# AdaLN block on one core: attention probabilities kept unsplit in fp32, context and row sums on column tiles of 32

## Chip, core and metric

The kernel runs on one core of a Trainium2 chip. The metric is the time of one execution on the device in microseconds (us). The measured times are the median of three runs, 688.05 us, with 682.75 and 689.03 us as the lowest and highest.

## What is computed

The reference is one transformer block with adaptive layer norm on x of shape (8, 512, 256). Cut to what matters:

```python
mod = (silu(c) @ wmod).reshape(8, 6, 1, 256)      # shift, scale and gate, twice
h = layernorm(x) * (1 + ca) + sa
# inner block, 16 heads of 16 columns, window of 128 keys
g = layer_norm(h, ln1)
q, k, v = g @ Wq + bq, g @ Wk + bk, g @ Wv + bv
scores = einsum('blhd,bmhd->bhlm', q, k) * 0.25 + bias   # key j allowed where i-128 <= j <= i
attn = softmax(scores)
ctx = einsum('bhlm,bmhd->blhd', attn, v)
h = h + ctx @ Wo + bo
h = h + gelu(layer_norm(h, ln2) @ W1 + b1) @ W2 + b2     # 256 -> 1024 -> 256
x = x + ga * h
# second half: layer norm, shift and scale, mix with the previous token, then
out = sigmoid(xr @ Wr.T) * (square(relu(xk @ Wk.T)) @ Wv.T)
x = x + gb * out
```

## The kernel before

The five engines each run an instruction list written out by hand; semaphores tie them together. TensorE is called PE below, VectorE DVE, ScalarE ACT, GpSimd POOL, and SP is the queue that issues most transfers.

**Units.** The work is cut into 16 units `u` (8 batches times 2 halves of the heads) and, for the later layers, 16 half batches `i`. One unit of attention has four calls `gp = 4u + j`. Each call holds two heads: the key axis of a stationary tile interleaves the two heads (even partitions for one, odd for the other), so 64 keys of two heads fill 128 partitions. A call's scores fill eight key tiles `s`, each seen by a window of up to 192 queries, 1344 query columns in all. They lie with keys on partitions and queries along the row, unnormalised.

**One call before.** `scores(gp)` on PE (split fp16 operands stacked along the contraction, L325) writes PSUM; `exps` on ACT (L874, L879) writes `p32[gp % 2]` in fp32; `select` on POOL (L1927 to L1932) zeroes what is outside the window; `high_p` on ACT (L889) rounds it to fp16 as `p_hi`; `low_p` (DVE L1373 for j = 0 and 3, POOL L1940 for j = 1 and 2) writes the rest `p_lo`. `context(gp)` on PE (L350) multiplies 28 blocks of 128 x 128 probabilities, as the stationary operand, with 66 or 34 columns of `v_blk`, which holds the fp16 halves of v and a column of ones for the row sums. The output has queries on partitions. `normalise(gp)` on DVE (L1384, L1385, L1390) inverts the row sums, adds the two halves and writes `cx`. After four calls `transposes_c(u)` on PE (L361, four fp32 transposes of 128 columns) and `context_t(u)` on ACT (L914) turn `cx` into `ct` with channels on partitions, which `out_project` (L377) reads. v itself is split by `split_v` (ACT L859) and `rest_v` (DVE L1346).

**Maxima.** `maxima(u, qt)` finds a bound for the exponent. It issues fp16 products on 32 x 32 tiles: row tile j, column tile qb. For qt = 0 the first loop (L289) gives 256, 192, 128 and 64 columns for qb = 0 to 3 (four products each, one per j), the second loop (L293) 64, 128, 192 and 256, in this order:

```python
tiles = [(qt * P + qb * QB, quad[qb * QB:(qb + 1) * QB, j, :], slice(2 * HD * j, 2 * HD * (j + 1)))
         for qb in range(4) for j in range(HQ)]
```

**Buffers that couple the engines.** There are two slots of `p32`, `p_hi` and `p_lo`. Four PSUM banks (`quad`, the ring `ring_s`) are shared by projections, values, scores, maxima (which take all four), and transposes. The ring `ring_c` is one bank, for the context. `ring_b` and `ring_f` serve the later layers.

**Order.** Between the start-up (about the first 200 us) and the drain, a loop over batches interleaves scores, maxima and contexts of one unit with `up`, `down`, `receptance`, `keys` and `values_b` of earlier half batches. `warm` issues matmuls on an identity (L230) that fill waits in the start-up. On SP, `stacks(u)` issues 24 transfers of q and k per unit (L2163, L2165), `load_v` four per half (L2174).

## Time and profile before

| | |
|---|---|
| median of 3 runs | 688.05 us |
| profiled execution | 686.02 us, span 684.3 us |
| PE busy | 589.2 us (86%) |
| DVE busy | 509.6 us (74%) |
| ACT busy | 508.7 us (74%) |
| POOL busy | 366.8 us (54%) |
| granted TensorE clock, mean | 0.974 of 2.4 GHz |

PE's busy time counts the modelled end of every matmul, which reaches past the start of the next, so the pace of a stream of matmuls is read from start to start, not from the mean duration. The clock was at half speed only in stretches of the first 200 us and at the very end (0.88 on average in the first 100 us, 1.00 from 200 us to 600 us). Waits are named by the instruction that waited and the one that released it. Two times are used for a transfer: the time its issue takes on the queue, and the time from issue to landing.

### The profile page before, as it was taken

To read this page: it belongs to the slowest core of one execution; us is meant where nothing else is said; L and a number is where in the kernel's file an instruction comes from. 1 tells how busy PE (TensorE), PEld (TensorE's weight loads), DVE (VectorE), ACT (ScalarE), POOL (GpSimd) and SP (SyncE) were. 2 spreads that over 40 slices of the span, in tenths; PEclk is the share of its full clock that TensorE was granted. 3 is DMA by queue.
4 is the path that set the end of the run, shared out by engine and by line. 5 is a ranking of instruction groups with operands and counts; after the bars stand their busy time and mean duration, and the time that the engine had idled before them with its cause. 6 is when DMAs were issued, how large, how long until landed. Compare 5 with 4: busy or idle time off the path is not lost.

```text
span 684.3 us, 18053 instructions
## 1 busy us (share of the span) xinstructions
PE 589.2 (86%) x6814; PEld 470.4 (69%) x6814; DVE 509.6 (74%) x1058; ACT 508.7 (74%) x780; POOL 366.8 (54%) x514
## 2 busy tenths in 40 slices
PE   5686697998789898899889898989898988899986
PEld 2555586877577676767676767677777766777775
DVE  5576577777788788788888888888987687564563
ACT  2623755579698979897989888998898886894642
POOL 5202444481639554865677475937593657564231
PEclk9878999999999999999999999999999999999999
DMA  3734212232023032403232223222311332101010
GB/s 129 276 72 102 64 43 48 62 100 67 19 67 98 18 89 55 117 24 86 65 79 72 73 66 82 80 60 64 76 57 46 73 72 64 32 2 48 31 39 32
DMA packets 56867, 47.05 MB, mean 69 GB/s; under 512 B 26235, under 2 KB 48061, under 8 KB 56782
## 3 DMA queue, kind: packets, MB, share of 16 engines
q1 hardware_dynamic: 53798, 43.85, 23.9%
q10 hardware_dynamic: 2984, 2.05, 1.2%
q8 instruction: 55, 0.90, 0.6%
q14 instruction: 30, 0.25, 0.1%
HBM read 18.11 MB, written 4.23 MB: 33 GB/s over the span
## 4 chain that ended last, share of the span: by engine, by line
PE 39%; ACT 29%; issue 10%; DVE 9%; SPq 7%; DMA 3%; POOL 2%; ACTq 0%; DVEq 0%; POOLq 0%
ACT bank L942 6%; ACT p L874 5%; SPq L2163 4%; PE bank L230 4%; SPq L2165 4%; ACT hid_hi L952 3%; PE bank L425 3%; PE bank L463 3%; PE bank L451 3%; PE bank L426 3%; PE bank L427 3%; ACT L942 3%; PE quad L325 3%; ACT kt_hi L846 2%; DVE nmax L1359 2%
## 5 line engine op out<-in xcount | busy, mean ns | idle before, releaser
L1927 POOL TENSOR_SCALAR_AFFINE_SELECT p<-p 128x448 f32<-128x448 f32 x64 | 40.4, 632 | 218.7 <-ACT p L874 179.1
L874 ACT ACTIVATE p<-quad,scale_s 128x768 f32<-128x768 f32 (+1 forms) x102 | 81.9, 821 | 39.6 <-PE quad L325 28.5
L889 ACT ACTIVATE p_hi<-p 128x1344 f16<-128x1344 f32 x64 | 83.9, 1322 | 14.3 <-POOL p L1932 7.1
L1940 POOL TENSOR_TENSOR p_lo<-p,p_hi 128x1344 f16<-128x1344 f32 x32 | 87.6, 2736 | 5.0 <-ACT p_hi L889 5.0
L325 PE MATMUL quad<-q_st,k_st 100*128 100x192 f16 (+3 forms) x576 | 61.4, 229 | 22.4 <-ACT p L874 7.6
L1359 DVE TENSOR_REDUCE nmax<-quad 128x8 f32<-128x1032 f32 x64 | 78.9, 1234 | 2.2
L408 PE MATMUL bank<-bt_hi,w_hi 128*128 128x256 f16 x256 | 70.5, 275 | 9.5 <-DVE hid_lo L1432 8.3
L1432 DVE SCALAR_TENSOR_TENSOR hid_lo<-bank,inv_f,hid_hi 128x512 f16<-128x512 f32 x64 | 48.0, 749 | 37.8 <-ACT hid_hi L952 37.6
L425 PE MATMUL bank<-w_hi,hid_hi 128*128 128x256 f16 x256 | 70.0, 274 | 0.9 <-DVE hid_lo L1432 0.8
L409 PE MATMUL bank<-bt_lo,w_hi 128*128 128x256 f16 x256 | 70.2, 274 | 0.0
L410 PE MATMUL bank<-bt_hi,w_lo 128*128 128x256 f16 x256 | 70.2, 274 | 0.0
L942 ACT ACTIVATE bank<-bank,bias,scale_g 128x256 f32<-128x256 f32 x128 | 63.5, 537 | 8.6 <-PE bank L410 8.4
L426 PE MATMUL bank<-w_lo,hid_hi 128*128 128x256 f16 x256 | 69.8, 273 | 0.0
L427 PE MATMUL bank<-w_hi,hid_lo 128*128 128x256 f16 x256 | 69.8, 273 | 0.0
L325 PEld LDWEIGHTS quad<-q_st,k_st 100*128 100x128 f16 x576 | 42.7, 97 | 37.9 <-issue 11.1
L350 PE MATMUL bank<-v_blk,p_hi 128*128 128x66 f16 x896 | 55.2, 195 | 2.3 <-DVE cx L1390 1.4
L350 PE MATMUL bank<-v_blk,p_lo 128*128 128x34 f16 x896 | 57.0, 181 | 0.0
L1356 DVE COPY_PREDICATED quad<-later,quad 128x248 f32<-128x248 int16 x64 | 26.7, 417 | 37.9 <-PE quad L293 37.6
L350 PEld LDWEIGHTS bank<-v_blk,p_hi 128*128 128x128 f16 x896 | 45.2, 97 | 8.2 <-issue 4.3
L1373 DVE TENSOR_TENSOR p_lo<-p,p_hi 128x1344 f16<-128x1344 f32 x32 | 49.6, 1549 | 1.2 <-ACT p_hi L889 1.2
L230 PE MATMUL bank<-ident 128*128 128x128 f32 x322 | 50.5, 313 | 0.0
L230 PEld LDWEIGHTS bank<-ident 128*128 128x128 f32 x322 | 45.7, 222 | 3.0 <-issue 1.9
(226 smaller groups left out, 1636.7 us busy)
## 6 DMA issues: line engine op xcount, KB each, us to landing
k_st<-kt_hi SPq DMA_DIRECT2D x120, 64.0 KB, 2.0
v_blk<-vn SPq DMA_DIRECT2D x64, 66.0 KB, 2.2
x<-x SPq DMA_DIRECT2D x16, 256.0 KB, 2.8
out<-x SPq DMA_DIRECT2D x16, 256.0 KB, 2.1
q_st<-qt_hi SPq DMA_DIRECT2D x120, 32.0 KB, 1.9
k_st<-kt_lo SPq DMA_DIRECT2D x60, 64.0 KB, 2.0
xa<-x SPq DMA_DIRECT2D x7, 512.0 KB, 4.5
stage<-w_ff SPq DMA_DIRECT2D x2, 1024.0 KB, 8.0
```

The source lines that it names most:

```text
L230: e.matmul(psum[5][:, 0:P], ident[:, :], ident[:, :], start=True, stop=True)
L325: last = e.matmul(bank[:, c0:c0 + w], k_st[0:MR, half, j, s * P:(s + 1) * P], q_st[0:MR, half, j, s * KW + q0:s * KW + q0 + w], start=True ...
L350: last = e.matmul(dst[:, :, v0:VW], p[:, c:c + P], v_blk[:, half, s, :, j * VW + v0:(j + 1) * VW], start=(i == 0), stop=(i == len(pieces) ...
L408: e.matmul(dst, w1_hi[:, k, ms], bt_hi[:, k, :], start=(k == 0), stop=False)
L425: e.matmul(dst, hid_hi[:, m, ts], w2_hi[:, m, :], start=(m == 0), stop=False)
L426: e.matmul(dst, hid_hi[:, m, ts], w2_lo[:, m, :], start=False, stop=False)
L427: last = e.matmul(dst, hid_lo[:, m, ts], w2_hi[:, m, :], start=False, stop=(m == MF - 1))
L874: e.activation(p32[gp % 2][:, c0:c0 + 2 * w].rearrange("p (n c) -> p n c", n=2), quad[:, b0:b0 + 2, 0:w], ACT.Exp, scale=scale_s[:, 1:2]). ...
L889: e.activation(p_hi[gp % 2][:, :].rearrange("p (n c) -> p n c", c=GW)[:, :, 0:QW], p32[gp % 2][:, :].rearrange("p (n c) -> p n c", c=QW), ...
L942: e.activation(dst, dst, ACT.Gelu_apprx_tanh, bias=bias_1[:, m:m + 1], scale=scale_g[:, 0:1]).then_inc(s_gl, 1)
L1359: e.tensor_reduce(nmax[:, :, :, qt].rearrange("p a j -> p j a"), quad[:, :, 2 * QB - 2:2 * WIN].rearrange("p j (c a) -> p j a c", a=2), AX ...
L1940: e.tensor_tensor(cut(p_lo), p32[gp % 2][:, :].rearrange("p (n c) -> p n c", c=QW), cut(p_hi), ALU.subtract).then_inc(s_plp, 1)
```

## The change

Probabilities are no longer split. `high_p`, both `low_p`, `split_v`, `rest_v`, `normalise`, `transposes_c` and `context_t` are gone, and so are `p_hi`, `p_lo` and `cx`; `p32` has six slots. The roles of the operands in `context` are exchanged: v is the stationary operand (128 x 32, fp32), the probabilities are streamed (fp32, up to 192 columns at a time), and the output has channels on partitions already. `context(q)` handles a pair of calls. Its two value products write partitions 32j to 32j+31 of one bank, that is column tile j of the array, for two of the four j; the two products with `sel` (ones, for the row sums of each head, repeated over 16 rows) write the other two column tiles in a bank of `ring_s`.

The row sums then go a long way: `copy_den` (ACT) to SBUF, `fold_den` (SP, a transfer that lays one row of every 16 out as 128 x 32), `divide` (DVE, reciprocal), `save_den` (SP, to DRAM), `spread_den` (SP, back to 128 x 512, each row repeated 16 times), and `scale_c` (DVE) multiplies the context bank by it into `ct`. `scale_c` frees the one context bank. `copy_v` (ACT, two instructions per two token tiles) replaces the split of v. All five engines' lists are written in a new order, and the weights' columns for v and Wo's rows are reordered on the host.

```diff
-    VW = 2 * HD + 1
+    VW = 4 * HD
+    SLOTS = 6
...
+        den_rows = nc.dram_tensor("den_rows", (NU, 8, L), F32, kind="Internal").ap()
...
-        vn = sb("vn", [P, NT, 4, HQ * VW], F16)
-        v_blk = sb("v_blk", [P, 2, 8, 2, HQ * VW], F16)
+        vn = sb("vn", [P, NT, 2, 2, 2 * VW])
+        v_blk = sb("v_blk", [P, 2, 8, 2 * VW])
...
-        p32 = [sb(f"p32_{i}", [P, PW]) for i in range(2)]
-        p_hi = [sb(f"p_hi{i}", [P, 7 * GW], F16) for i in range(2)]
-        p_lo = [sb(f"p_lo{i}", [P, 7 * GW], F16) for i in range(2)]
-        rsum = sb("rsum", [P, NT, 2])
+        p32 = [sb(f"p32_{i}", [P, PW]) for i in range(SLOTS)]
...
-            def context(gp):
...
-                for t in range(NT):
-                    dst = bank[:, t * 2 * VW:(t + 1) * 2 * VW].rearrange("p (a w) -> p a w", a=2)
...
-                        last = e.matmul(dst[:, :, v0:VW], p[:, c:c + P], v_blk[:, half, s, :, j * VW + v0:(j + 1) * VW],
-                                        start=(i == 0), stop=(i == len(pieces) - 1))
...
+            def context(q):
...
+                if pair == 0:
+                    bank, free = ring_c.take(("av", u), s_ct, u + 1)
+                    e.wait_ge(s_vin[half], 4 * DMA * (u // 2 + 1))
+                    hold(e, *free)
+                den, free = ring_s.take(("den", q), s_dc, q + 1)
...
+                e.wait_ge(s_sel, 2 * q + 2)
                 hold(e, *free)
...
+                for s in (0, 3, 6, 1, 2, 4, 5, 7):
+                    c, w = {6: (6 * QW + KW, 2 * KW), 7: (6 * QW, KW)}.get(s, (s * QW, QW))
+                    for i in range(2):
+                        j = 2 * pair + i
+                        e.matmul(bank[32 * j:32 * j + 32, s * KW:s * KW + w], v_blk[:, half, s, 2 * j * HD:2 * (j + 1) * HD],
+                                 p32[(2 * q + i) % SLOTS][:, c:c + w], start=(s == 0), stop=(s == 7))
+                    for i in range(2):
+                        j = (2 * pair + i + 2) % HQ
+                        last = e.matmul(den[32 * j:32 * j + 32, s * KW:s * KW + w], sel[:, :],
+                                        p32[(2 * q + i) % SLOTS][:, c:c + w], start=(s == 0), stop=(s == 7))
                 last.then_inc(s_av, 1)
-
-            def transposes_c(u):
...
+            def copy_den(q):
...
+                rows = slice(0, 64) if q % 2 else slice(64, 128)
+                e.wait_ge(s_av, q + 1)
+                hold(e, s_rc, DMA * (q - 1))
+                e.activation(dn[rows, :], ring_s.at["den", q][rows, :], ACT.Copy).then_inc(s_dc, 1)
...
-                if first == 0 and gp >= 2:
-                    e.wait_ge(*low_of(gp - 2))
+                if first == 0:
+                    hold(e, s_av, (gp - SLOTS) // 2 + 1)
...
-            def high_p(gp):
...
-            def context_t(u):
...
-            def normalise(gp):
...
+            def divide(u):
...
+                e.wait_ge(s_rc, 2 * DMA * (u + 1))
+                e.reciprocal(rc[:, :], rc[:, :]).then_inc(s_rr, 1)
+
+            def scale_c(u):
...
+                e.wait_ge(s_rb, DMA * (u + 1))
+                hold(e, s_wo, 2 * (u // 2))
+                e.tensor_tensor(ct[:, u % 2, :], ring_c.at["av", u][:, :], rb[:, :], ALU.mult).then_inc(s_ct, 1)
...
+            def fold_den(q):
...
+                e.wait_ge(s_dc, q + 1)
+                hold(e, s_rs, DMA * u)
+                e.dma_start(rc[64 * pair:64 * pair + 64, :], dn[r0:r0 + 64:HD, :]).then_inc(s_rc, DMA)
+
+            def save_den(u):
...
+                e.wait_ge(s_rr, u + 1)
+                e.dma_start(den_rows[u], rc[:, :]).then_inc(s_rs, DMA)
+
+            def spread_den(u):
...
+                e.wait_ge(s_rs, DMA * (u + 1))
+                hold(e, s_ct, u)
+                e.dma_start(rb[:, :], den_rows[u].rearrange("r (o c) -> r o c", o=1).broadcast_to([8, HD, L])).then_inc(s_rb, DMA)
```

**Where instructions stand.** PE before, in the loop over batches: one context call with what stands around it (up to 66 and 34 columns of v, 28 products).

```order
L377 MATMUL quad<-wo,ct 128x256 x4
L350 MATMUL bank<-v_blk,p_hi 128x66 x2
L350 MATMUL bank<-v_blk,p_lo 128x2x17 x2
L350 MATMUL bank<-v_blk,p_hi 128x66 x4
L350 MATMUL bank<-v_blk,p_lo 128x2x17 x4
L350 MATMUL bank<-v_blk,p_hi 128x66 x4
L350 MATMUL bank<-v_blk,p_lo 128x2x17 x4
L350 MATMUL bank<-v_blk,p_hi 128x66 x4
L350 MATMUL bank<-v_blk,p_lo 128x2x17 x4
L325 MATMUL quad<-q_st,k_st 128x192
L325 MATMUL quad<-q_st,k_st 128x96 x2
```

PE after, in the loop over batches: the end of the projection of one unit, `receptance`, and the first of the two context calls of a unit; `p_2` and `p_3` are two of the six probability slots.

```order
L252 MATMUL quad<-at_hi,wa_lo 128x512
L439 MATMUL bank<-wb,mixed 128x256 x4
L318 MATMUL quad<-q_st,k_st 128x192 x4
L344 MATMUL bank<-p_2,v_blk 32x192
L344 MATMUL bank<-p_3,v_blk 32x192
L348 MATMUL quad<-p_2,sel 32x192
L348 MATMUL quad<-p_3,sel 32x192
...
L344 MATMUL bank<-p_2,v_blk 32x64
L344 MATMUL bank<-p_3,v_blk 32x64
L348 MATMUL quad<-p_2,sel 32x64
L348 MATMUL quad<-p_3,sel 32x64
L318 MATMUL quad<-q_st,k_st 128x192
```

Four products on four column tiles now stand behind each other, eight times per call; there are two such calls per unit where there were four calls and a group of transposes.

DVE before, in the loop: the three instructions of `normalise` stand behind each maximum or so; they wait for PE's context call (`av`).

```order
L1359 TENSOR_REDUCE nmax<-quad 128x4x2 [waits mov]
L1384 RECIPROCAL rsum<-bank 128x8 [waits cx_s,av]
L1385 TENSOR_REDUCE bank<-bank 128x128
L1390 TENSOR_TENSOR cx<-bank,rsum 128x8x16 [waits ctr,cs]
L1444 SCALAR_TENSOR_TENSOR x<-bank,scale_y,x 128x512 [waits b2_s,f2]
```

DVE after: the reciprocal waits for two folding transfers (`rc_in`), the product for the spreading transfer (`rb_in`); three other instructions stand between, and the next maximum stands behind.

```order
L1536 RECIPROCAL rc<-rc 128x32 [waits rc_in]
L1568 TENSOR_TENSOR bt_lo<-bank,bt_hi 128x512 [waits bth]
L1595 SCALAR_TENSOR_TENSOR x<-bank,scale_y,x 128x512 [waits b2_s,f2]
L1649 SCALAR_TENSOR_TENSOR tr<-tr,bank 128x512 [waits r,vb]
L1543 TENSOR_TENSOR ct<-bank,rb 128x512 [waits wo_s,rb_in]
L1520 COPY_PREDICATED quad<-later,quad 128x4x62 [waits mxm,mtt]
L1523 TENSOR_REDUCE nmax<-quad 128x4x2 [waits mov]
```

SP after, in the loop: the two folds of a unit, the save and the spread, with the loads of v and of the gates between; the stacks of the next unit stand behind all of them.

```order
L2461 DMA rc<-dn 64x1x32 [waits rs,dc]
L2452 DMA v_blk<-vn 64x4x128 [waits av,v3]
L2452 DMA v_blk<-vn 64x4x128 x3
L2461 DMA rc<-dn 64x1x32 [waits rs,dc]
L2467 DMA den_rows<-rc 128x32 [waits rr]
L2491 DMA mod_g<-mod_rows 128x256 [waits yg,gates_out]
L2474 DMA rb<-den_rows 128x1x512 [waits ct_s,rs]
```

Four transfers per unit (two folds, save, spread) are new on this queue.

## Rows read from the trace of the kernel before

**Rows 1.** The page, part 1: busy time, share and instructions of each engine.

```profile
PE 589.2 (86%) x6814; PEld 470.4 (69%) x6814; DVE 509.6 (74%) x1058; ACT 508.7 (74%) x780; POOL 366.8 (54%) x514
```

**Rows 2.** The page, part 4: the chain that ended last, shares by engine.

```profile
PE 39%; ACT 29%; issue 10%; DVE 9%; SPq 7%; DMA 3%; POOL 2%; ACTq 0%; DVEq 0%; POOLq 0%
```

**Rows 3.** Windows, one batch of the loop: busy us and counts, clock, DMA.

```profile
283.00:353.70 70.70, 64.26 (x810) 50.90 (x794) 60.36 (x124) 61.75 (x96) 45.33 (x63) 1.00 0.27 70
```

**Rows 4.** Waits of PE: instruction, releaser, total us, times, longest.

```profile
PE quad L293 <- ACT p L874: 12.7, 19, 1.1
PE bank L408 <- DVE hid_lo L1432: 8.3, 16, 1.4
PE quad L325 <- ACT p L874: 7.6, 13, 0.9
...
PE quad L361 <- DVE cx L1390: 6.5, 9, 1.2
```

**Rows 5.** Timeline of PE: start, us; a context call and what follows.

```profile
297.21 0.23 PE L350 MATMUL bank<-v_blk,p_hi 128*128 128x66 f16 x2
...
298.08 0.29 PE L289 MATMUL quad<-kt_hi,qt_hi 32*32 32x256 f16 x16
```

**Rows 6.** Chain in order of time: four fp32 matmuls (256 columns); 16 on 128.

```profile
620.80 1.73 PE bank L451 x8
...
670.81 3.57 PE quad L235 x32
```

**Rows 7.** Groups by form, PE at 298.170 to 298.189: count, busy, mean ns.

```profile
L289 PE MATMUL quad<-kt_hi,qt_hi 32*32 32x256 f16 x4 | 0.3, 278 | 0.0
L293 PE MATMUL quad<-kt_hi,qt_hi 32*32 32x256 f16 x3 | 0.3, 278 | 0.0
L289 PE MATMUL quad<-kt_hi,qt_hi 32*32 32x192 f16 x4 | 0.3, 252 | 0.0
L293 PE MATMUL quad<-kt_hi,qt_hi 32*32 32x192 f16 x4 | 0.3, 242 | 0.0
L289 PE MATMUL quad<-kt_hi,qt_hi 32*32 32x128 f16 x4 | 0.2, 225 | 0.0
L289 PE MATMUL quad<-kt_hi,qt_hi 32*32 32x64 f16 x4 | 0.2, 198 | 0.0
```

**Rows 8.** Groups by form, ACT: busy us, mean ns, idle before.

```profile
L889 ACT ACTIVATE p_hi<-p 128x1344 f16<-128x1344 f32 x64 | 83.9, 1322 | 14.3 <-POOL p L1932 7.1 <-DVE p_lo L1652 7.0
...
L942 ACT ACT_TABLE_LOAD x15 | 19.2, 1283 | 0.3
...
L859 ACT ACTIVATE vn<-quad 128x512 f16<-128x512 f32 x16 | 10.0, 624 | 7.3 <-PE quad L276 7.2
L914 ACT ACTIVATE ct<-quad 128x512 f32<-128x512 f32 x16 | 9.6, 603 | 0.8 <-PE quad L361 0.8
```

**Rows 9.** Groups by form, DVE: busy us, mean ns, idle before.

```profile
L1373 DVE TENSOR_TENSOR p_lo<-p,p_hi 128x1344 f16<-128x1344 f32 x32 | 49.6, 1549 | 1.2 <-ACT p_hi L889 1.2
...
L1385 DVE TENSOR_REDUCE bank<-bank 128x128 f32<-128x256 f32 x64 | 24.4, 381 | 0.0
...
L1390 DVE TENSOR_TENSOR cx<-bank,rsum 128x128 f32<-128x128 f32 x64 | 18.6, 291 | 2.2
...
L1384 DVE RECIPROCAL rsum<-bank 128x8 f32<-128x8 f32 x64 | 12.7, 198 | 10.8 <-PE bank L350 10.7
...
L1346 DVE TENSOR_TENSOR vn<-quad,vn 128x512 f16<-128x512 f32 x16 | 11.0, 692 | 6.3 <-ACT vn L859 5.3
```

**Rows 10.** The page, part 5, POOL: busy us, mean ns, idle before.

```profile
L1940 POOL TENSOR_TENSOR p_lo<-p,p_hi 128x1344 f16<-128x1344 f32 x32 | 87.6, 2736 | 5.0 <-ACT p_hi L889 5.0
```

**Rows 11.** DMA issues: count, KB each, median us from issue to landing.

```profile
v_blk<-vn SPq DMA_DIRECT2D x64, 66.0 KB, 2.2
...
mod_a<-mod_rows SPq DMA_DIRECT2D x7, 256.0 KB, 4.7
```

**Rows 12.** Timeline of SP: start, us, issues of stacks; two are merged.

```profile
320.69 1.22 SPq L2165 DMA_DIRECT2D k_st<-kt_hi  x2
```

More of the change, by code:

```diff
@@ L592, in _ @@
+            project(2)
             context(0)
[L593 to L594 removed]
             scores(2, 0, 2)
             scores(2, 2, 4)
[L597 to L609 removed]
@@ L682, in _ @@
[L682 to L700 removed]
+            maxima(4, 2)
@@ new lines, in _ @@
+            values(2, 1)
+            scores(17, 0, 2)
+            context(6)
+            context(7)
+            up(1, 0, 1)
+            down(0, 0)
+            maxima(5, 0)
+            down(0, 1)
+            up(1, 1, 2)
+            maxima(5, 1)
+            up(1, 2, 3)
+            scores(17, 2, 4)
+            up(1, 3, 4)
+            scores(18, 0, 2)
+            scores(18, 2, 4)
+            scores(19, 0, 2)
+            scores(19, 2, 4)
+            context(8)
+            out_project(2)
@@ L701, in _ @@
+            scores(22, 2, 4)
+            up(2, 0, 1)
+            maxima(6, 1)
+            up(2, 1, 2)
+            out_project(3)
+            values(3, 0)
+            for b in range(3, 7):
+                u = 2 * b
+                gp = 8 * b
+                q = 4 * b
+                up(u - 4, 2, 3)
                 maxima(u, 2)
-                down(u - 4, 1)
+                up(u - 4, 3, 4)
                 scores(gp - 1, 0, 2)
                 values(b, 1)
-                scores(gp - 1, 2, 4)
@@ new lines, in _ @@
+            receptance(9)
+            scores(NG - 8, 2, 4)
+            scores(NG - 7, 0, 2)
+            down(10, 1)
+            maxima(NU - 1, 0)
+            transposes_b(11)
+            values_b(9)
+            scores(NG - 7, 2, 4)
+            up(11, 0, 1)
+            maxima(NU - 1, 1)
+            up(11, 1, 2)
+            out_project(NU - 4)
+            scores(NG - 6, 0, 2)
+            up(11, 2, 3)
+            context(2 * NU - 4)
+            up(11, 3, 4)
+            maxima(NU - 1, 2)
```

1576 lines of the change are left out of this document (939 added, 637 removed).

## Prediction, made before the changed kernel was run

> **What bounds the kernel now.** I read the page first. PE is the busiest engine at 86%, with DVE and ACT at 74% and POOL at 54% [rows 1]. That busy time includes modelled ends, so it shows where to look and not how full PE is. The chain of work that ended last runs over PE for 39%, over ACT and DVE for 38% together, and SP's queue and transfers take 10% [rows 2]: no engine bounds the kernel alone. Next the windows: one batch of the loop lasts 70.7 us, in which PE is busy for 64.3 us, ACT for 61.8, DVE for 60.4 and POOL for 45.3, at the full granted clock of 2.4 GHz [rows 3]. Then the waits of PE: it mostly waits for ACT (exponentials, 12.7 and 7.6 us) and for DVE's low half of the hidden layer (8.3 us), in many short pieces, and 6.5 us at the transposes of the context [rows 4]. In all PE is idle for 684.3 - 589.2 = 95.1 us [rows 1]. So a change is worth what it adds to PE's stream, less what it takes off the lists of ACT and DVE that PE waits for.
>
> **What leaves PE.** A context call takes from 297.21 to 298.08, 0.87 us, to the next instruction [rows 5]; 64 calls are 55.7 us. The 64 transposes of 128 fp32 columns go at the pace of the identity matmuls, 3.57 / 32 = 0.112 us [rows 6]: 7.2 us. Together 62.9 us.
>
> **What comes to PE.** Four fp32 matmuls of 256 columns leave eight records and take 1.73 us [rows 6], so an fp32 product is two passes one behind the other, each 0.216 us, or 0.844 ns per column. The new call streams 1344 columns four times, in two passes each: 1344 x 8 x 0.844 ns = 9.07 us if nothing overlaps. It is spread over four column tiles: 2.27 us if all four run side by side, 4.54 if two do. The trace has no fp32 product on a column tile; its nearest rows are the maxima, fp16 products on tiles of 32 x 32. Sixteen of 256 columns and less, and seven of the sixteen behind them, are in flight together at 298.19 [rows 7]. More telling is the order: L293's products stand in the program with 64 columns first, then 128, 192 and 256 (four each, one row of tiles after the other). Yet by 298.189 seven have started, all of 192 and 256 columns, while those of 64 and 128, which stand ahead of them, are missing: their tiles still hold L289's products of 256 and 192 columns [rows 7]. A product that waits for its own tile does not hold back a later one on another. That is what the new call needs, since the second pass of each product waits for its own first pass. The Trainium skill ("TensorE: Matmul & The Clock Gate", Part 3, the mechanism) says the opposite, that matmuls start and end in strict program order. By that rule the second pass would hold back the next tile and the sum would take 4.54 us per call; it is rival B, and rows 7 speak against it. I take 2.27 plus 0.38 for what doesn't overlap: the last key tile has only 64 columns for eight weight loads, the tiles start one after the other, and the array changes its tiling before and after. That is a choice, about a sixth of the stream; the bounds are 2.27 and 9.07. So 2.65 us per call, 32 calls, 84.8 us. PE's stream grows by 84.8 - 62.9 = 21.9 us.
>
> Weight loads: 64 per call, of 32 fp32 columns. A load of 128 fp32 columns is hidden under 0.112 us [rows 6], so by columns one costs at most 0.028 us and 64 cost 1.8 us, under the stream. If a load costs the full 0.112 us whatever its width and none overlap, they take 7.2 us per call (rival C). The Trainium skill ("TensorEngine Tiling (Array Packing)", Restrictions) adds that column tiling turns fast weight loading off; for fp32 weights no row here tells that apart.
>
> **What leaves the other engines.** ACT: 64 x 1.322 us for the high half, plus 10.0 and 9.6 us [rows 8], 103.5 us. It gets 32 copies of row sums at about the 0.60 us of L914 and 32 strided half-width copies of v at about 0.4 us (19 + 13 us), and its order has 42 table loads for 30, 12 x 1.28 us = 15 us [rows 8]. Net about -56 us, 6 of the 61.8 us per batch. DVE loses 49.6 + 24.4 + 18.6 + 12.7 + 11.0 = 116.3 us and gets 16 reciprocals (0.2 us) and 16 products (0.69 us, as L1346), 14 us [rows 9]: about 11 us less per batch. POOL loses 87.6 us [rows 10]. In the loop ACT and DVE fall to some 56 and 49 us a batch against PE's list; with six slots instead of two the exponentials can also run ahead.
>
> What this is worth on the path: the 6.5 us at the transposes go with them [rows 4]. Of the three largest queue waits, 12.7 + 8.3 + 7.6 = 28.6 us [rows 4], I take 22, since the maxima still wait for PSUM banks that the exponentials free. In the start-up PE isn't the bound (warm-up matmuls fill it). About 17 of the 64 calls stand there; each sheds 1.32 on ACT, 0.87 on DVE and half the time 1.55 more, 2.97 us; 17 calls are 50 us, of which the chain's 38% [rows 2] is 19. Table loads and copies give some 4 back: -15 us.
>
> **The row sums' detour.** After a unit's second call: copy 0.6, fold 0.6 (issue, half of 1.22 [rows 12]) + 2.2, reciprocal 0.2, save 0.6 + 2.2, spread 0.6 + 4.7 (as the transfer of 256 KB into 128 rows [rows 11]), product 0.7: 12.4 us. Until `scale_c` the only context bank is taken, so the next unit's first call is behind it. In the loop PE's shorter stretch between those two calls is about 96 of the 444 rows that a batch has in the new order, 96 / 444 x 70.7 = 15.3 us; the longer stretch and `out_project` have more. So it is covered by 3 us, not by much. Behind the waiting product on DVE stands the next maximum, behind that PE's scores: DVE has three instructions (0.7 us each) between reciprocal and product in one of two places, against 8 us of transfers. PE's own list reaches that maximum only about 9 us after the call, so I price the rest at 3 us in all. On SP the next unit's stacks stand behind save and spread, which hold the queue until a transfer has landed; four more issues per unit are 5 us in a batch whose some 64 issues take 40 us, and the stacks are wanted most of half a batch later. Nothing for that.
>
> **Sum.** 684.3 + 21.9 - 6.5 - 22 - 15 + 3 = 665.7 us of span; 686.02 - 684.3 = 1.7 us lie outside: 667.4. The median of the runs stood 2.0 us above the profiled execution but one of its three runs was below it; I say 668 us.
>
> **Rivals.**
> A, the forecast (0.70): four tiles side by side, other lists shorter. With 2.27 us per call (-12), all 28.6 us of waits gone (-6.6) and a better start-up it reaches 640; with nothing gained from waits (+22) and the start-up (+15) 704. Its own range is 645 to 690.
> B, two tiles at a time (0.13): 4.54 + 0.38 us per call is 2.27 x 32 = 72.6 us more; PE is then the bound and absorbs about 15 us of what idles: 668 + 58 = 726. For it: no fp32 product on column tiles in the trace. Against it: rows 7. It decides from 3.3 us per call on, where the 20 us of gain are spent.
> C, weight loads or no overlap (0.07): 7.2 us per call gives 668 + 32 x 4.55 = 814, 9.07 us some 870. Against it: 23 products on small tiles in flight at once [rows 7].
> D, the detour decides (0.10): if it takes over 15.3 us, each further us stalls PE about 14 times in the loop. At 2 us over it is +28, 696 us; with less, 675 to 690. For it: two SP waits for a landing and other transfers in between; against it: the durations above.
>
> **Chances.** "Within 1%" is about what a measurement can't tell from no change. Faster (below 681): 0.61 from A, 0.03 from D, 0.64. Same: 0.06 + 0.04 = 0.10. Slower: 0.03 + 0.13 + 0.07 + 0.03 = 0.26. The range 640 to 704 leaves out B and C, 0.20.
>
> **What would show it.** Right: a call takes 2.4 to 3.0 us from its first L344 to the next instruction, with starts on four tiles within a few ns; the batch falls from 70.7 to 67 to 69 us; ACT near 56 and DVE near 49 us per batch; the waits for exponentials under 8 us. Wrong: calls of 4.5 us or more (B, C); PE waiting at L344 for `ct` or at the maxima for DVE behind the spread transfer (D); a start-up no shorter though the lists are.

## The result, and the profile after

The changed kernel takes 702.46 us (median of 4 runs, 701.29 to 704.54), the kernel before 687.99 us in the same session (682.75 to 689.03). The ratio is 1.0229, with a 95% interval of 1.0172 to 1.0286: slower, by 12 to 20 us; whether by more than 2% is open. The forecast was 668. Where a kernel had runs more than 1.5% above its fastest, ratios and intervals leave them out, while medians are of all runs. The span of the profiled execution is 699.5 us, before 684.3; the mean granted clock is 0.961 of 2.4 GHz, before 0.974.

First the page's part 1 and the chain by engine, of the changed kernel; they answer to [rows 1] and [rows 2].

```profile
PE 609.8 (87%) x7006; PEld 479.4 (69%) x7006; DVE 422.4 (60%) x847; ACT 460.5 (66%) x767; POOL 260.7 (37%) x482
...
PE 53%; DVE 16%; ACT 12%; issue 9%; DMA 5%; POOL 4%; SPq 1%; ACTq 0%; DVEq 0%; POOLq 0%
```

ACT, DVE and POOL have shed 48, 87 and 106 us (forecast: 56, 102 and 88). DVE's share of the chain has risen from 9% to 16%, on an engine that is busy 60% of the time. Three batches of the loop, in the columns of [rows 3]:

```profile
291.50:365.70 74.20, 67.31 (x824) 51.76 (x823) 49.85 (x98) 56.75 (x96) 32.62 (x58) 0.98 0.30 85
365.70:439.80 74.10, 67.25 (x822) 51.95 (x822) 49.73 (x98) 56.81 (x96) 32.51 (x58) 0.98 0.31 85
439.80:515.80 76.00, 68.27 (x819) 52.84 (x818) 49.87 (x98) 56.61 (x96) 32.32 (x58) 0.96 0.31 82
```

A batch takes 74.1 to 76.0 us for 70.7, and the clock, 1.00 before, is 0.96 to 0.98. The loop is also where the time is lost. From the start of the scores of unit 7 to that of unit 15, four batches, the windows of before (first) and after are

```profile
294.60:578.50 283.90, 254.67 (x3158) 201.36 (x3157) 234.95 (x466) 242.90 (x373) 178.25 (x242) 1.00 0.26 67
```

```profile
291.10:590.20 299.10, 268.50 (x3306) 207.34 (x3305) 189.36 (x363) 225.78 (x376) 120.41 (x218) 0.97 0.30 80
```

15.2 us more, which is the whole difference of the spans; the start-up is 3.5 us shorter and what follows unit 15 is 3.5 us longer. PE's idle time in these four batches is 29.2 us before and 30.6 after: what the shorter lists and the missing transposes took off, other waits put back. The waits of PE answer to [rows 4]:

```profile
PE quad L318 <- DVE nmax L1523: 17.9, 16, 2.1
PE quad L286 <- DVE nmax L1523: 11.0, 12, 2.1
PE quad L300 <- DVE nmax L1523: 8.9, 6, 2.0
...
PE quad L318 <- ACT p L964: 4.2, 6, 1.9
PE bank L396 <- DVE hid_lo L1583: 2.6, 3, 1.4
PE quad L286 <- ACT p L964: 2.6, 4, 1.2
```

The three groups that the forecast looked at have fallen from 28.6 us to 4.2 + 2.6 + 2.6 = 9.4 us (scores L318, maxima L286 and the hidden layer's L396 are L325, L293 and L408 of before). At the head of the list stands something else: 37.8 us of waits for `nmax`, DVE's reduction behind each `maxima`. In the kernel before these rows were

```profile
PE quad L293 <- DVE nmax L1359: 5.5, 3, 2.2
PE quad L325 <- DVE nmax L1359: 2.6, 8, 0.7
...
PE quad L243 <- DVE nmax L1359: 2.4, 2, 2.0
...
PE quad L274 <- DVE nmax L1359: 1.1, 1, 1.1
```

11.6 us in all. One such place, in the timeline of PE of the changed kernel (start, duration, line, shape, count, idle time before and what ended it; the first row stands for several alike):

```profile
299.69 0.27 PE L398 MATMUL bank<-bt_hi,w_lo 128*128 128x256 f16 x1
300.74 0.36 PE L286 MATMUL quad<-kt_hi,qt_hi 32*32 32x320 f16 x16 [0.79 <-DVE nmax L1523]
303.11 0.49 PE L318 MATMUL quad<-q_st,k_st 100*128 100x192 f16 x4 [2.00 <-DVE nmax L1523]
303.43 3.19 PE L365 MATMUL quad<-wo,ct 128*128 128x256 f32 x8
```

and DVE at the same time:

```profile
301.27 0.42 DVE L1520 COPY_PREDICATED quad<-later,quad 128x248 f32<-128x248 int16 x1 [0.53 <-PE quad L286]
301.73 1.23 DVE L1523 TENSOR_REDUCE nmax<-quad 128x8 f32<-128x1032 f32 x1
```

`maxima` fills all four score banks; DVE reads them for 0.42 + 1.23 us, and with the hand-overs 2.37 us pass between PE's maxima and the scores behind them. DVE isn't late: it was itself idle ahead of the maxima. It is a round trip, and only what PE has to do between `maxima` and the next user of a score bank can hide it. Before, calls that use other banks mostly stood there in the loop: a context call, a piece of `up` or `down`, `keys` or `receptance`. In the second half of the new loop `up(u - 2, 1, 2)` alone stands between the first two maxima (0.79 us of wait are left), and scores stand directly behind the second: 2.00 us.

The last row of PE's timeline shows more: eight passes of L365, the same work as those of 1.73 us in [rows 6], take 303.43 to 306.42, 2.99 us. The window of that stretch:

```profile
303.90:307.30 3.40, 3.40 (x14) 2.53 (x13) 2.27 (x7) 2.05 (x4) 1.33 (x4) 0.50 0.51 170
```

The granted clock is 0.50, that is 1.2 GHz, right behind two waits of 0.79 and 2.00 us. It isn't so each time: the place comes once per batch, with the same waits to 0.01 us, and behind it the clock fell in two of four batches (here and at 451 us) and stayed in the other two, as at 377 us:

```profile
377.30:380.00 2.70, 2.58 (x17) 1.98 (x17) 2.49 (x7) 2.35 (x4) 1.07 (x3) 1.00 0.55 191
```

From 200 to 600 us the windows of before (first) and after show 1.00 and 0.97:

```profile
200.00:600.00 400.00, 358.88 (x4388) 284.69 (x4386) 326.96 (x660) 342.24 (x526) 254.23 (x345) 1.00 0.26 67
```

```profile
200.00:600.00 400.00, 360.56 (x4300) 278.71 (x4294) 255.82 (x494) 301.41 (x504) 167.63 (x305) 0.97 0.30 80
```

The new call itself does what the forecast said. Timeline of PE, first passes and second passes of its first four products and the instruction behind its last:

```profile
291.55 0.36 PE L344 MATMUL bank<-p,v_blk 128*32 128x192 f32 x2
291.56 0.36 PE L348 MATMUL quad<-p,sel 128*32 128x192 f32 x2
291.73 0.33 PE L344 MATMUL bank<-p,v_blk 128*32 128x192 f32 x2
291.75 0.33 PE L348 MATMUL quad<-p,sel 128*32 128x192 f32 x2
...
293.96 0.30 PE L318 MATMUL quad<-q_st,k_st 100*128 100x192 f16 x2
```

Four products start within some 20 ns on four column tiles, their second passes 0.18 us later, and the call is over after 2.42 us (28 of the 32 calls; the others 2.28, 2.30, 3.70 and 4.77, of which the last two hold a wait or half clock).

### The profile page after: what moved, and what is told of

Read it like the earlier page. It is cut to its first block, busy times and chain, and to the rows that moved or that the text cites. A ratio compares the mean times of both kernels' runs of the same rounds, so it can differ in the third digit from the quotient of the medians.

```text
span 699.5 us, 18109 instructions
## 1 busy us (share of the span) xinstructions
PE 609.8 (87%) x7006; PEld 479.4 (69%) x7006; DVE 422.4 (60%) x847; ACT 460.5 (66%) x767; POOL 260.7 (37%) x482
## 4 chain that ended last, share of the span: by engine, by line
PE 53%; DVE 16%; ACT 12%; issue 9%; DMA 5%; POOL 4%; SPq 1%; ACTq 0%; DVEq 0%; POOLq 0%
PE bank L344 7%; DVE nmax L1523 5%; PE bank L223 4%; PE quad L318 4%; PE quad L365 3%; PE bank L439 3%; PE bank L463 3%; PE bank L451 3%; PE bank L413 2%; PE bank L414 2%; PE bank L415 2%; PE quad L286 2%; ACT bank L1015 2%; DVE mixed L1616 2%; PE bank L396 2%
## 5 line engine op out<-in xcount | busy, mean ns | idle before, releaser
L964 ACT ACTIVATE p<-quad,scale_s 128x576 f32<-128x576 f32 (+1 forms) x95 | 75.8, 804 | 34.0 <-PE quad L318 33.2
L344 PE MATMUL bank<-p,v_blk 128*32 128x192 f32 (+2 forms) x1024 | 80.1, 310 | 3.5 <-POOL p L2158 1.7
L318 PE MATMUL quad<-q_st,k_st 100*128 100x192 f16 (+3 forms) x576 | 59.6, 234 | 24.1 <-DVE nmax L1523 17.9
L348 PE MATMUL quad<-p,sel 128*32 128x192 f32 (+2 forms) x1024 | 80.0, 311 | 0.0
L396 PE MATMUL bank<-bt_hi,w_hi 128*128 128x256 f16 x256 | 70.1, 274 | 5.8 <-DVE hid_lo L1583 2.6
L344 PEld LDWEIGHTS bank<-p,v_blk 128*32 128x32 f32 x1024 | 58.5, 111 | 22.0 <-issue 7.1
L413 PE MATMUL bank<-w_hi,hid_hi 128*128 128x256 f16 x256 | 72.1, 282 | 1.2 <-DVE hid_lo L1583 1.2
L414 PE MATMUL bank<-w_lo,hid_hi 128*128 128x256 f16 x256 | 71.8, 280 | 0.0
L318 PEld LDWEIGHTS quad<-q_st,k_st 100*128 100x128 f16 x576 | 43.3, 100 | 39.5 <-issue 20.7
L348 PEld LDWEIGHTS quad<-p,sel 128*32 128x32 f32 x1024 | 57.1, 111 | 0.5
L1025 ACT ACTIVATE hid_hi<-bank,inv_f 128x512 f16<-128x512 f32 x64 | 43.2, 687 | 10.5 <-PE bank L415 6.3
L223 PE MATMUL bank<-ident 128*128 128x128 f32 x322 | 48.5, 304 | 1.3 <-DVE peak L1734 1.3
L969 ACT ACTIVATE p<-quad,scale_s 128x384 f32<-128x384 f32 (+1 forms) x66 | 33.8, 566 | 11.8 <-PE quad L318 11.8
```

The source lines that it names most:

```text
L223: e.matmul(psum[5][:, 0:P], ident[:, :], ident[:, :], start=True, stop=True)
L318: last = e.matmul(bank[:, c0:c0 + w], k_st[0:MR, half, j, s * P:(s + 1) * P], q_st[0:MR, half, j, s * KW + q0:s * KW + q0 + w], start=True ...
L344: e.matmul(bank[32 * j:32 * j + 32, s * KW:s * KW + w], v_blk[:, half, s, 2 * j * HD:2 * (j + 1) * HD], p32[(2 * q + i) % SLOTS][:, c:c + ...
L348: last = e.matmul(den[32 * j:32 * j + 32, s * KW:s * KW + w], sel[:, :], p32[(2 * q + i) % SLOTS][:, c:c + w], start=(s == 0), stop=(s == 7))
L396: e.matmul(dst, w1_hi[:, k, ms], bt_hi[:, k, :], start=(k == 0), stop=False)
L413: e.matmul(dst, hid_hi[:, m, ts], w2_hi[:, m, :], start=(m == 0), stop=False)
```

## The experiments

All ratios are to the kernel before, measured beside it on the same chip, with the 95% interval behind. "After" is 702.46 us (1.0229).

**The maxima's reduction made shorter, in both kernels.** This leaves out part of the computation: DVE takes the maximum over 94 of the 258 columns in each score bank, which holds two heads. The same line is changed in both (`short_max` of after and of before).

```diff
-                                quad[:, :, 2 * QB - 2:2 * WIN]...
+                                quad[:, :, 2 * P - 30:2 * WIN]...
```

> The changed kernel with DVE's maximum (L1523) over 94 of 258 columns per head pair: it leaves out part of the maximum, so the bound of the exponent is not the reference's. One reduction should fall from 1.23 us to about 0.6. Theory M (in the loop the changed kernel is held by the four-bank round trip of the maxima: products, copy, reduction, then the next user of these banks): PE's 38 us of waits for the reduction fall by at least 15 us, the half-clock stretches behind such waits get fewer, and the time falls by 12 to 25 us from 702 us. Rival S (PE's own longer stream, 2.42 us per context call, is what costs): waits shift elsewhere and the time falls by under 5 us.

> The same edit in the kernel before (part of the maximum is left out). Theory M: its waits for the reduction are only 12 us in all, PE waits for ACT instead, so the same 0.65 us per reduction off is worth under 8 us of 688, less than half of what it is worth in the changed kernel. Rival (the maxima's round trip held both kernels alike): the same gain in both.

Measured: after 677.53 us (0.9883, 0.9844 to 0.9921), before 674.92 us (0.9844, 0.9805 to 0.9884). The same edit gives 25 us in the changed kernel and 11 in the kernel before, less than half as expected, but more than the 8 us that I had set as its limit. In the changed one the waits at scores and maxima fall to

```profile
PE quad L318 <- DVE nmax L1523: 8.3, 7, 1.4
...
PE quad L286 <- DVE nmax L1523: 2.9, 3, 1.4
```

So with a short round trip the two kernels are 3 us apart instead of 14.5, though the stream of PE is as long as it was. Most of the loss hangs on the round trip's length. The edit also takes work off DVE, so it isn't yet proof that the wait is what matters.

**The row sums' detour taken out.** The kernel leaves out the division by the row sums: no fold, reciprocal, save and spread; `scale_c` multiplies by ones. One line of several is shown.

```diff
-                e.wait_ge(s_rb, DMA * (u + 1))
```

> The changed kernel without the row sums' way over DRAM: no fold, reciprocal, save and spread; the context is multiplied by a tile of ones, so the division by the row sums is left out. The products for the row sums and their copy stay. Theory D (the detour of some 12 us and its place on SP and DVE costs time where it is): 6 to 15 us less than 702 us. Theory M: the detour is covered in this order, under 4 us less, since DVE waits only 7.5 us for the spread and 5.7 us for the fold.

Measured: 698.44 us (1.0205, 1.0164 to 1.0247), by the medians 4 us and by the ratios 2 us less than with it, which the intervals don't tell from nothing. The detour was priced at 3; rival D, by which it decides, falls. The figure is net: with the detour gone PE waits 8.0 us for the stacks of k, half of it in this row and half in one for `kt_lo`, where the changed kernel has no such row.

```profile
PE quad L318 <- DMA k_st<-kt_hi: 4.0, 2, 2.0
```

**The order of the tiles.** The same 64 passes, all key tiles of one column tile first.

```diff
-                for s in (0, 3, 6, 1, 2, 4, 5, 7):
-                    for i in range(2):
+                for i in range(2):
+                    for s in (0, 3, 6, 1, 2, 4, 5, 7):
```

> The changed kernel with the same 32 products per context call in another order: all eight key tiles on one column tile, then the next, where the changed kernel goes round the four column tiles for each key tile. Nothing is left out. If four tiles overlap only because neighbours in the program sit on different tiles: a call takes 6.8 to 9.1 us instead of 2.42 us and the kernel 840 to 910 us. If the array finds work for idle tiles however deep it stands in the list: a call still takes about 2.4 us and nothing changes.

One run: 876.4 us. Timeline of PE, one call and what follows it:

```profile
296.45 4.07 PE L344 MATMUL bank<-p,v_blk 128*32 128x192 f32 x29
...
304.47 0.28 PE L415 MATMUL bank<-w_hi,hid_hi 128*128 128x256 f16 x1
```

8.02 us per call for 2.42, and 32 x 5.6 = 179 us, which covers the whole 174 us. Here tiles overlap when neighbours in the program lie on different tiles. With eight products for one tile in a row, they stand in line, and what is behind them with them.

**A first other order.** `receptance(u-4)` behind the second maxima, with ACT's `gate(u-4)` moved accordingly, and `down(u-3, 1)` in two halves around transposes and scores.

```diff
+                down(u - 3, 1, 0, MF // 2)
                 transposes_a(b + 1)
                 scores(gp + 3, 0, 2)
-                down(u - 3, 1)
+                down(u - 3, 1, MF // 2, MF)
...
-                receptance(u - 4)
...
                 maxima(u + 2, 1)
+                receptance(u - 4)
                 scores(gp + 5, 0, 2)
```

> The changed kernel, only its calls in another order. Receptance (the outline's u-4) stands behind the second maxima instead of ahead of the first down half, and down(u-3, 1) is cut into two halves, one on each side of the transposes and of the scores, so that no user of a score bank stands directly behind the maxima; the same at the end of the kernel. Work per engine is unchanged. Theory M (the loss sits in PE waiting for the maxima's reduction, 17.9 + 11.0 + 8.9 = 37.8 us in the changed kernel where the kernel before had 11.6): these waits fall to 10 to 18 us, the time falls by 15 to 25 us from 702, to 677 to 687 us. Theory E (the new call is simply longer on PE than what left it, the order doesn't matter): the waits move elsewhere, the time stays within 4 us of 702.

Measured: 717.36 us (1.0381, 1.0324 to 1.0438), by the medians 15 us and by the ratios 10 us slower, instead of 15 to 25 faster. Its waits:

```profile
PE bank L439 <- DVE hid_lo L1586: 17.4, 5, 4.3
PE quad L286 <- DVE nmax L1526: 10.4, 11, 2.1
PE quad L318 <- DVE nmax L1526: 8.3, 10, 2.1
```

The waits for `nmax` did fall, from 37.8 to 22.0 us (10.4 + 8.3 + 3.3, the last at the transposes). But receptance takes a bank that the hidden layer holds until `hid_lo`, and now waits 4.3 us for it in a place that holds up the scores.

**Matmuls that only fill.** Order as in the changed kernel; eight identity matmuls behind the second maxima, six ahead of the transposes.

```diff
                 maxima(u + 2, 1)
+                fill(u - 2, 0, 8)
                 scores(gp + 5, 0, 2)
```

> The changed kernel in its own order, with identity matmuls of 128 columns into the hidden layer's free PSUM bank: eight behind the second maxima, six ahead of the transposes, where PE waits for the maxima's reduction (14 x 0.11 us = 1.5 us per batch, some 20 us in all if none of it were hidden in waits). Theory clock (the stalls cost mostly because the clock is granted at half speed behind them, 27 us of such stretches in the loop): those stretches go and the time falls by 8 to 12 us, to 690 to 694 us. Theory stall (the waits themselves are the cost): the time stays at 700 to 706 us, with the half-clock stretches gone or not.

Measured: 695.46 us (1.0138, 1.0095 to 1.0180): 7 us less, from matmuls that compute nothing. From 200 to 600 us:

```profile
200.00:600.00 400.00, 372.68 (x4534) 291.17 (x4532) 258.89 (x502) 309.15 (x517) 174.35 (x324) 0.99 0.31 82
```

0.02 of 400 us is 8 us at full clock. The fills don't shorten the round trip, they only fill it, so in the loop some 7 us of the loss are carried by the clock. (In the first 100 us the clock is no help to the comparison: it was 0.88 in the profiled execution of before, 0.91 after and 0.83 here.)

**The score bank of the row sums.** The first pair's row sums go to free rows of the context's bank; `receptance` and `gate` stand between the two context calls for it, and the second call waits for the copy of the first one's sums.

```diff
-                den, free = ring_s.take(("den", q), s_dc, q + 1)
+                if pair == 0:
+                    den, free = ring_c.at["av", u], (s_dc, 0)
```

> The changed kernel, with the first pair's row sums in the free part of the context's own PSUM bank, instead of in a bank of the four that scores and maxima share; receptance and gate stand between the two context calls. If the context call's need of a score bank is what holds PE and the maxima up (the ring of four banks is the bottleneck), the waits for the maxima's reduction fall by 8 us or more and the time falls by 5 to 12 us, to 690 to 697 us. If it is only the order of the calls, the time stays within 3 us of 702.

Measured: 706.85 us (1.0307, 1.0252 to 1.0362), 4 us slower, which the intervals don't tell from nothing; the waits for `nmax` hardly change (16.0, 11.4 and 8.8 us). So taking one of the two context calls off the score banks doesn't help, at least with the moves that it needed.

**Before, without the context calls behind the maxima.**

```diff
+                context(gp - 6)
+                context(gp - 5)
                 maxima(u, 0)
-                context(gp - 6)
                 up(u - 4, 1, 2)
-                context(gp - 5)
```

> The kernel before, with only its order changed: the two context calls of a batch, which stand behind maxima calls, are put ahead of them. Work is unchanged. Theory M says that these calls covered the maxima's reduction: PE's waits for the row maxima rise from 11.6 us to 20 to 30 us, and the time rises by 5 to 15 us, to 691 to 701 us. If the cover was worth nothing, the time stays within 3 us of 686.

Measured: 721.78 us (1.0514, 1.0474 to 1.0554), and not for the reason that I gave. Its waits:

```profile
PE bank L408 <- DVE hid_lo L1432: 21.7, 16, 2.0
PE bank L350 <- DVE cx L1390: 21.1, 12, 2.1
...
PE quad L293 <- DVE nmax L1359: 5.7, 4, 2.2
```

The `nmax` waits hardly moved (a piece of `up` still covers them). Two calls side by side wait for the one context bank, and `up` for its own. So this says nothing on the cover of the maxima; it says that the order of before holds 36 us together by keeping users of one bank apart.

**A second other order.** A context call between the two maxima, a piece of `up` behind the second, the first pair's row sums as above; ACT's and DVE's lists follow.

```diff
                 maxima(u + 2, 0)
-                up(u - 2, 1, 2)
+                context(q)
                 maxima(u + 2, 1)
+                up(u - 2, 1, 2)
                 scores(gp + 5, 0, 2)
+                context(q + 1)
```

> The changed kernel with another order and nothing left out: in the second half of the loop the first pair's context call stands between maxima(u+2, 0) and maxima(u+2, 1) as a cover of 2.4 us, and up(u-2, 1, 2) stands behind maxima(u+2, 1) ahead of the scores; so that this call needs no score bank, its row sums go to the free rows of the context's bank. down(u-3, 1) is cut in two halves around the transposes. Receptance stays where the changed kernel has it. Theory M: the waits for the maxima's reduction (37.8 us in the changed kernel) fall to 15 to 22 us, none of them longer than 1 us in the second half of the loop, half-clock stretches in the loop fall under 15 us, and the time falls by 12 to 22 us, to 680 to 690 us. If it only moves waits, 698 us or more.

Measured: 733.70 us (1.0672, 1.0600 to 1.0744). The waits for `nmax` fell to 22.9 us (12.8 + 6.9 + 3.2), and again another took their place:

```profile
PE quad L318 <- DVE x L1562: 21.4, 4, 5.4
```

The scores wait for the out-projection's bank, which DVE's list frees 5.4 us late, once per batch. What DVE itself waits for there was not taken apart further.

**The reduction in two halves**, in the changed kernel, in the second order, and in the kernel before. DVE reduces first the two banks that PE takes next, and each half signals by itself. Nothing is left out, the lists stay as they are, and DVE has more to do, not less.

```diff
-                e.tensor_reduce(nmax[:, :, :, qt]..., quad[:, :, ...]...).then_inc(s_mx, 1)
+                for two in (ring_s.at["first", u, qt], 1 - ring_s.at["first", u, qt]):
+                    js = slice(2 * two, 2 * two + 2)
+                    e.tensor_reduce(nmax[:, :, js, qt]..., quad[:, js, ...]...).then_inc(s_mx, 1)
```

> The changed kernel, in its own order, with DVE's reduction of four score banks (1.23 us) cut into two of two banks each, and the pair that PE wants next first. Nothing is left out. PE gets its next bank some 0.6 us earlier behind each maxima call. Theory M: the 34 waits of 37.8 us shrink by 0.3 to 0.5 us each, and some half-clock stretches go with them: 8 to 18 us less than 702, 684 to 694 us. If the round trip isn't what costs, the 64 extra instructions on DVE leave the time at 700 to 706 us.

> Both edits together (the order of the first kernel of this job, and the reduction cut in two). If the round trip of the maxima is the one cause of the loss, the two overlap: the sum is less than of both apart, the waits for the reduction are under 12 us, and the time comes to 676 to 686 us, at or below the kernel before. If it is two independent causes, the gains add up: below 676 us.

> The kernel before with DVE's reduction cut in two in the same way. Its DVE is busy for 60.4 us per batch and its waits for the reduction are 11.6 us. Theory M says that the round trip mattered less there: 2 to 6 us less than 686, or nothing, as DVE's queue is fuller (680 to 687 us). If the cut gains as much here as in the changed kernel (8 us or more), the round trip isn't what the new order lost.

Measured: changed kernel 692.59 us (1.0066, 1.0032 to 1.0100), second order 731.43 us (median of four runs; the ratio, 1.0550, 1.0470 to 1.0631, rests on two of them), kernel before 684.53 us (0.9983, 0.9953 to 1.0012). The waits of the changed kernel with it:

```profile
PE quad L321 <- DVE nmax L1528: 10.7, 18, 1.5
PE quad L289 <- DVE nmax L1528: 10.6, 12, 2.1
...
PE quad L303 <- DVE nmax L1528: 6.7, 5, 1.5
```

37.8 us have become 28.0, and the time is 10 us less; in the kernel before the same edit gives nothing that can be measured. As the edit adds to DVE's work, it is the wait and not DVE's load that the changed kernel suffers from. In the second order it changes nothing that can be told from the spread of the runs (721.88 to 737.04 us).

**The forecast's relief by itself.** The kernel before, in which the halves of the probabilities are converted for one of seven column groups only; the rest of the halves keeps older values, so most of that conversion is left out. ACT's line is shown; the subtractions on DVE and POOL are cut alike.

```diff
-                e.activation(p_hi[gp % 2][:, :]...[:, :, 0:QW],
+                e.activation(p_hi[gp % 2][:, :]...[:, 0:7 if gp < 2 else 1, 0:QW],
```

> The kernel before, with the high and low halves of the probabilities converted for one of seven column groups only (192 of 1344 columns; the rest of the halves keeps older values), so ACT, DVE and POOL shed most of the work that the change takes from them, some 60, 40 and 70 us, while PE's stream and every list keep their order. This prices one step of the prediction by itself. If shorter lists are worth what the prediction gave (22 us of queue waits and 15 us in the start-up for somewhat larger reliefs), the time falls by 20 to 30 us, to 656 to 666 us. If PE's waits for other engines stand mostly on the chain of one item (a product, its exponential or gelu, the next product) and not on how full the lists are, it falls by less than 10 us, and the waits for the exponentials stay above 18 of 20 us (12.7 + 7.6 before).

Measured: 681.23 us (0.9947, 0.9908 to 0.9987): 4 us less, where the forecast's pricing wants 20 to 30. The batch of [rows 3] again, and the waits:

```profile
283.00:353.70 70.70, 64.53 (x804) 51.49 (x803) 54.74 (x126) 54.92 (x97) 34.22 (x63) 1.00 0.28 73
```

```profile
PE quad L293 <- ACT p L874: 12.7, 19, 1.1
PE bank L408 <- DVE hid_lo L1432: 9.1, 15, 1.4
...
PE quad L325 <- ACT p L874: 5.3, 10, 0.9
```

ACT has 54.92 us of work in that stretch for 61.75, DVE 54.74 for 60.36 and POOL 34.22 for 45.33 (of the relief that the change brings in the loop: all of ACT's, half of DVE's, most of POOL's). From the scores of unit 7 to those of unit 15 it takes 283.0 us for 283.9; 2.9 of the 4.9 us by which its span is shorter are gained ahead of that. The maxima wait for the exponentials exactly as before: 12.7 us, 19 times, at most 1.1 us. A place of that kind, ACT and then PE:

```profile
305.08 0.74 ACT L874 ACTIVATE p<-quad,scale_s 128x576 f32<-128x576 f32 x1
```

```profile
306.08 0.36 PE L293 MATMUL quad<-kt_hi,qt_hi 32*32 32x320 f16 x16 [1.09 <-ACT p L874]
```

PE's scores lie at 304.32 to 304.98 in the same timeline, ACT takes them at 305.08 and needs 0.74 us. The wait is one item's way through one instruction. The same place in the kernel before, where PE's scores end at 307.84:

```profile
307.95 0.74 ACT L874 ACTIVATE p<-quad,scale_s 128x576 f32<-128x576 f32 x1
```

```profile
308.97 0.36 PE L293 MATMUL quad<-kt_hi,qt_hi 32*32 32x320 f16 x16 [1.12 <-ACT p L874]
```

From 200 to 600 us the maxima of the kernel before have 16 such waits, and in all 16 the exponential starts 0.09 to 0.11 us after the scores' end. ACT isn't idle there (at 5 of the 16 it has only just finished the exponential before), but this item doesn't queue.

**One move alone.** Only `down(u-3, 1)` in halves (the first hunk of the first order, with the same at two places outside the loop).

> The changed kernel with one move only: down(u-3, 1) cut in two halves around the transposes of the next batch and the scores behind them (the same at two places outside the loop). Both earlier reorderings held this move beside others. Theory M: the wait at the transposes for the maxima's reduction falls from 8.9 to about 3.3 us (as it did in the earlier two), nothing takes its place, and the time falls by 4 to 8 us, to 694 to 699 us. If every reordering costs more than it brings, 702 us or more.

Measured: 702.09 us (1.0263, 1.0194 to 1.0333), no gain where 4 to 8 us were expected. The transposes' wait for `nmax` fell from 8.9 to 3.3 us as expected. In its place the next maxima, which now come sooner behind the scores, wait for exponentials (2.6 us before the move), and L451 for `mixed` (1.8 us before it):

```profile
PE quad L286 <- ACT p L967: 7.0, 8, 1.2
...
PE bank L451 <- DVE mixed L1619: 4.7, 5, 2.0
...
PE quad L300 <- DVE nmax L1526: 3.3, 4, 2.0
```

**Three edits together:** reduction in two, `down` in halves, six filling matmuls.

> The changed kernel with the three edits that don't reach into other lists: the reduction cut in two, down cut in halves around the transposes, and six identity matmuls behind the second maxima. Nothing is left out. If the round trip and the clock behind it are the loss, the gains (10, about 5, and some 4 of the fill's 7 us) add up: 680 to 686 us, level with the kernel before. If they overlap almost wholly, 690 us or more.

Measured: 690.81 us (median of ten runs; the ratio, 1.0035, 1.0000 to 1.0069, rests on seven of them), where 680 to 686 had been hoped for, from 200 to 600 us at a granted clock of 1.00. It is the best full version of the changed kernel that was run, level with or a little above the kernel before, and no better, within what can be told, than with the cut reduction alone. No version that computes everything beat the kernel before by a margin that can be measured.

## Why the prediction was wrong

**The cost on PE was right, and on the high side.** Rival A's mechanism holds: four column tiles side by side, 2.42 us per call for 2.65 forecast (2.27 plus 0.38). The stream grew by 32 x 2.42 - 62.9 = 14.5 us, not 21.9. The weight loads are hidden. Rivals B and C are out: 28 of 32 calls take 2.42 us, and in the one above 4.5 the instruction behind it waits for 2.31 us. Doubting strict program order was sound: the second pass of one tile doesn't hold back the next tile. But the sentence drawn from [rows 7], that a product waiting for its own tile doesn't hold back a later one on another, is too wide. There one product stood waiting per tile; with eight in a row for one tile (8.02 us per call) they do hold back the rest. The program must alternate tiles, a condition that the forecast did not name and the new kernel meets.

**The loads were right in the loop.** ACT 56.75 us and DVE 49.85 us per batch for 56 and 49; over the whole run ACT shed 8 us and DVE 15 us less than forecast. The 6.5 us at the transposes of the context are gone. The detour costs 2 to 4 us net for 3.

**The step that failed is "what this is worth on the path".** It gave 22 of 28.6 us of waits and 15 us of the start-up to shorter lists. The experiment `light_halves` gives most of ACT's relief and half of DVE's alone: 4 us, and the largest wait unchanged to the tenth. The waits of [rows 4] are short (12.7 us in 19 pieces, none over 1.1), and I read them as queues. They were latencies of single items: scores, one exponential of 0.74 us, next maxima. Taking work off ACT elsewhere doesn't shorten that. (This is shown for the maxima's waits for exponentials. Of the other two groups only the sizes in `light_halves` are known: 5.3 us for 7.6 at the scores, 9.1 for 8.3 at `hid_lo`.) A queue would have shown in ACT, which at all 16 places started on that very item 0.1 us after PE's scores ended; I had not looked at when the releaser began. In the changed kernel these three waits did fall, by 19.2 us. Which part of that is the new order, the six slots, or PE being held up at `nmax` instead, no run tells apart; PE's idle time fell by only 5.4 us in all (95.1 to 89.7).

**The start-up gained 3.5 us for 15.** PE began the scores of unit 7 at 294.6 us before and 291.1 after, with the same share of `up` and `down` done (25% each) and two context calls fewer. The clock alone can account for that: in the first 100 us it was 0.91 in this execution for 0.88, 3 us. At the scores of unit 9 (365.3 and 365.2) the first batches of the loop had used the lead up. The share of the chain (38%) by which I weighed 50 us of shed work prices the path with latencies in it as if all of it shrank with the load.

**The wait that took the place of the ones removed.** The sum had no term for what the new order does to `maxima`. The change moved the context calls away from behind them, as each now needs a score bank itself and, with all four taken by the maxima, can't stand there without waiting too. The waits for `nmax` rose by 26 us. I had named "the maxima still wait for PSUM banks" as a reason to take 22 and not 28.6, but for the banks that exponentials free; nothing was priced for the banks that the maxima hold themselves. Two edits of the round trip bear it out: 25 against 11 us, and 10 against some 2 that can't be told from nothing.

**The clock had no term either.** By the mean granted clocks, 699.5 x 0.039 = 27.3 us of PE's full-speed time are lost after and 684.3 x 0.026 = 17.8 us before: 9.5 us. From 200 to 600 us alone it is 0.03 of 400, 12 us; the start-up was 3 us better. That is an upper estimate, since it counts the clock of stretches in which PE idles: PE's busy time rose by 20.6 us, of which 6.1 are left beside the stream's 14.5. `fill` gives 7 back.

Put together for the spans: +14.5 (stream) + 9.5 (clock), which leaves 15.2 - 24.0 = -8.8 us for everything else. That everything else was forecast at -6.5 - 22 - 15 + 3 = -40.5. With 6.1 us for the clock it is -5.4, the fall of PE's idle time. The 32 to 35 us between are the failed step, partly for relief that never was there, partly spent again on the round trip; the experiments don't split it further. Open stays, too, whether some order of the five lists hides the round trip without a new wait: both reorderings tried were worse (717 and 734 us), and one clean move came out even.

The measured time lies near 704, the forecast's own bound for nothing gained from waits and start-up. That is in part luck: the stream was 7 us cheaper than in that sum, and the lost clock and the waits for `nmax` weren't in it.

Of the signs that the forecast named, those for the call and the loads came (calls of 2.42 us, loads of ACT and DVE). Those for its gain did not: batches of 74 to 76 us, not 67 to 69, and of its signs of being wrong, "a start-up no shorter though the lists are" came nearly true. "Waits for the exponentials under 8 us" came true (4.2 + 2.6 = 6.8 us) and meant nothing, since others grew.

## What to carry to other kernels

Before counting a wait as relief, look at when its releaser began: if it took up the item at once, the wait is latency, and only other work between the two, or a shorter instruction, takes it away. When an edit gives a call a new bank or moves it, ask what the call was covering where it stood. And in lists this tight a single move has to be priced with what it uncovers: three reorderings here, all with the same cut of `down` in them, made their target's wait shorter and the kernel no faster.

## What the runs showed of the hardware

- fp32 products with 128 x 32 weights on four column tiles run side by side: 64 passes in 2.42 us, 8.02 us when the program goes through one tile after the other. Their weight loads (64 per call, mean 111 ns) don't show in the 2.42 us, of which one tile's stream is 2.27 by [rows 6].
- The clock: between 200 and 600 us of the changed kernel each of six stretches at 1.2 GHz stood behind one to three waits of PE of 1.8 to 3.2 us together, as at 303.90:307.30 behind 0.79 and 2.00 us; a stream of fp32 passes then takes 2.99 us for 1.73. The same pair of waits was followed by half clock in two of four batches, so the waits alone don't settle it. The kernel before, with waits of up to 1.5 us in that stretch, had none there. Matmuls on an identity in two of these waits brought the clock of 200 to 600 us from 0.97 to 0.99 and 7 us. Forecasts of a new wait of 2 us should hold that second price, as a chance and not as a certainty.
